# Attention by spectra: context relative to its last row, float32r pair spectra of the two halves, a new order on TensorE

## The chip, the cores and the metric

One core of a Trainium2 chip. A core has five instruction streams: TensorE (PE: matrix products; its weight loads are PEld), VectorE (DVE), ScalarE (ACT), GpSimd (POOL) and SyncE (SP), which here only issues transfers. The metric is device time in microseconds; runs of the same program agree within about 0.05% here. Products land in PSUM, eight banks of 128 x 512 fp32.

## The reference

Inputs: x and a context, both (8, 512, 2048), a 2048 x 2048 weight with bias, and low-rank adapters.

1. q = layernorm(x). In 8 heads of 256 positions each, for every column: corr = ifft(fft(q) * conj(fft(ctx))).real along the positions, its 12 largest lags, a softmax of them, and out[pos] = sum over lags of weight * ctx[min(lag + pos, last)]. The first line of the result is x + out.
2. y = x + layernorm(x) @ W + bias + adapters, in a second stage.

The clipped index min(lag + pos, last) makes positions beyond the end read the last row of the context again. The kernel computes the sum over lags as a second correlation, over a sequence of twice the length: the context, and behind it its last row repeated.

```
w, idx = top_k(corr, topk); w = softmax(w)
for i in range(topk):
    g = minimum(idx[..., i] + pos, L - 1)
    out = out + w[..., i] * take_along_axis(v, g, axis=2)
```

## The kernel before

After a short first stage come the attention stage (some 1,750 us) and the feed-forward stage (some 1,560 us).

**Attention stage.** The work is 32 groups, four to a batch, of 512 positions x 512 columns. All transforms are products with tables: a sequence is folded (sum and difference of its halves) and each fold multiplied with a cosine and a sine table. Four kinds of spectra result, ER, EI, OR and OI (even and odd frequencies, real and imaginary), one PSUM bank each. For one group:
- `fold_v`, `fold_z` (L493 to 509, GpSimd): the folds of the context, and of its second half with the last row (`vrow`, loaded 128 times over).
- `v_spectrum`, `z_spectrum` (L756, L774, TensorE): 8 fp32 products of 512 columns each, through `forward` (L742); v goes to banks 0 to 3, z to 4 to 7. `store_spectrum` (L627, ScalarE) keeps them in `spe` and `spo`.
- `normalise`, `fold_q`, `high_of_q`, `rest_of_q`: q is normalised, folded and cut into two f16 parts; `q_spectrum` (L765) is 24 f16 products.
- `corr_products_even/odd` (VectorE, q spectra times v spectra), `corr_sums` (GpSimd), `turn_row` (ScalarE, one row's sign), `correlation` (L805, TensorE, 16 fp32 products of 256 columns), `corr_to_sbuf` (ScalarE).
- `top_lags` (L958, VectorE): two sums, maxima and replacements for the largest lags; `exponentials`, `sums_of_top`, `divide_w` on ScalarE between; at the end four `wd` products, the weights by lag.
- `transpose_w` (L783), `transposed_out` and `w_rest` (two f16 parts), `weight_spectra` (L793, 48 f16 products into all eight banks), `out_products` (L925, VectorE, nine products in two halves), `out_sums` (L534, GpSimd), `output` (L818, 16 fp32 products of 512 columns), `add_output` (L989).

Each engine runs a step n, one group's share, in an order written out by hand; nothing plans it, and engines meet only through semaphores. A step handles group n and, ahead of it, parts of groups n+1, n+2 and n+3. TensorE (L830): q of n+1, transposes of n, z of n+1, weight spectra of n, correlation of n+1, v of n+2, output of n. VectorE (L996): `w_rest` n, correlation products n+1, row statistics, [weight rest, half 0], output products n, `top_lags` n+1, `add_output` n, [weight rest, half 1, or the largest weight]. The parts in brackets are the side work of the feed-forward weight: in steps 0 to 15 VectorE finds its largest value (L883), in steps 16 to 31 ("convert") it is turned into two f16 parts. For that ScalarE casts (`weights_high`, L681), VectorE subtracts (`weights_rest`, L874), and SP stores both parts and loads the next half (L449 to 459); there is one buffer `wc`. A GpSimd operation and a VectorE operation that reads two SBUF tiles do not run at the same time in this trace, which the rows of line 876 below show by their lengths.

SP (L435) issues every transfer in one order as well, and a wait in it holds up what is behind it: inputs for n+3, the row for the statistics, in the convert steps the two weight stores and loads, then after `out_add` the store of the group's result, its landing, and the load of the next residual.

**Feed-forward stage.** 32 tiles of 128 rows. Per tile: statistics (VectorE), normalise (ScalarE), transposes, the adapters and 192 f16 products of 512 columns (TensorE), the bias added by GpSimd (`prepare`, L1140), and results added by VectorE.

## Time and profile before

| | |
|---|---|
| median of three runs | 3445.23 us (3444.69 to 3445.47) |
| the profiled execution, its time | 3438.6 us |
| its span, first to last instruction | 3436.8 us |
| mean granted TensorE clock | 0.983 |
| busy TensorE, VectorE, ScalarE, GpSimd | 3280.5, 2006.3, 931.3, 1574.0 us |

Busy times are sums over both stages. TensorE's records overlap, since a product is entered before the one ahead of it has drained, so the distance between two starts is the cost of a product, not the length of its record. An fp32 product has two records. What a change in a stage is worth is read from the stage's own timeline, which is why nearly all the rows below are of single groups.

### The profile page before, as it was taken

What the parts mean: (1) busy time and instruction counts of PE and PEld (TensorE: products, weight loads), DVE (VectorE), ACT (ScalarE), POOL (GpSimd) and SP (SyncE); (2) the same over time, 40 slices, a digit from 0 to 9 for tenths busy, and PEclk for the clock granted to TensorE, in tenths of its full rate; (3) what the DMA queues carried; (4) which work ended last, traced back from release to release, by engine and by line L of the source; (5) the groups of instructions that cost most, each with busy time, mean ns of one, the idle gap of its engine ahead of it and who ended that gap; (6) DMA issues with size and microseconds to landing.
All of it is one profiled execution on the core that took longest, in us unless ns stands there. A gap on an engine that the chain in (4) does not pass through costs nothing. (4 is left out here: it accounts for less than half of the span.)

```text
span 3436.8 us, 38078 instructions
## 1 busy us (share of the span) xinstructions
PE 3280.5 (95%) x14592; PEld 1639.7 (48%) x14592; DVE 2006.3 (58%) x2768; ACT 931.3 (27%) x1559; POOL 1574.0 (46%) x727
## 2 busy tenths in 40 slices
PE   7699999999999999999995999999999999999999
PEld 4354554554544455455542444444444444444444
DVE  4289989999888999998985232232323232232321
ACT  1434444344334444544432110111101110111100
POOL 0587888878868888887862110111001110111000
PEclk9799999999999999999998999999999999999999
DMA  7133243342342334234223611011110111011110
GB/s 310 70 113 132 98 153 110 119 153 100 129 152 108 140 127 177 103 126 147 84 101 124 228 50 59 37 38 59 50 54 29 59 49 59 37 38 59 50 50 25
DMA packets 125328, 335.59 MB, mean 98 GB/s; under 512 B 7648, under 2 KB 24160, under 8 KB 108800
## 3 DMA queue, kind: packets, MB, share of 16 engines
q1 hardware_dynamic: 125184, 333.64, 27.1%
q8 instruction: 94, 1.54, 0.2%
q14 instruction: 50, 0.41, 0.0%
HBM read 245.27 MB, written 88.34 MB: 97 GB/s over the span
## 5 line engine op out<-in xcount | busy, mean ns | idle before, releaser
L1248 PE MATMUL ps<-w_hi,h_hi 128*128 128x512 f16 x2048 | 780.0, 381 | 18.4 <-issue 16.9
L1250 PE MATMUL ps<-w_hi,h_lo 128*128 128x512 f16 x2048 | 779.1, 380 | 0.0
L1249 PE MATMUL ps<-w_lo,h_hi 128*128 128x512 f16 x2048 | 778.9, 380 | 0.0
L1143 POOL TENSOR_TENSOR rp<-ve,half 128x1 f32<-128x1 f32 x32 | 17.6, 549 | 1243.7 <-DVE ve L1301 1243.7
L1355 DVE SCALAR_TENSOR_TENSOR xt<-ps,w_back,xt 128x512 f32<-128x512 f32 x128 | 96.0, 750 | 757.1 <-PE ps L1250 756.1
L826 PE MATMUL ps<-op,it 128*128 128x512 f32 x1024 | 448.1, 596 | 21.0 <-DVE op L956 21.0
L752 PE MATMUL ps<-wt,fp 128*128 128x512 f16 x1536 | 339.1, 381 | 9.9 <-ACT spo L639 6.9
L1248 PEld LDWEIGHTS ps<-w_hi,h_hi 128*128 128x128 f16 x2048 | 200.9, 98 | 258.0 <-issue 27.2
L826 PEld LDWEIGHTS ps<-op,it 128*128 128x128 f32 x1024 | 195.7, 191 | 267.8 <-issue 262.3
L1250 PEld LDWEIGHTS ps<-w_hi,h_lo 128*128 128x128 f16 x2048 | 201.0, 98 | 243.9 <-issue 3.9
L1249 PEld LDWEIGHTS ps<-w_lo,h_hi 128*128 128x128 f16 x2048 | 201.0, 98 | 228.9 <-issue 3.3
L1179 ACT ACTIVATE axT<-ps 128x128 f16<-128x128 f32 x32 | 8.9, 277 | 884.4 <-PE ps L1253 884.4
L752 PEld LDWEIGHTS ps<-wt,fp 128*128 128x128 f16 x1536 | 150.7, 98 | 203.2 <-issue 20.4
L814 PE MATMUL ps<-it,cp 128*128 128x256 f32 x1024 | 232.7, 386 | 9.3 <-DVE vlast L946 5.3
L745 PE MATMUL ps<-cg,ft 128*128 128x512 f32 x512 | 230.2, 592 | 0.0
L814 PEld LDWEIGHTS ps<-it,cp 128*128 128x128 f32 x1024 | 194.3, 192 | 50.8 <-DVE vlast L946 15.8
L541 POOL TENSOR_TENSOR mr<-mr 128x1024 f32<-128x1024 f32 x64 | 151.3, 2364 | 142.1 <-DVE mr L940 142.1
L545 POOL TENSOR_TENSOR op<-mr 128x512 f32<-128x512 f32 x64 | 204.7, 3198 | 0.0
L1147 POOL TENSOR_TENSOR xt<-xt,brow 128x2048 f32<-128x2048 f32 x32 | 144.6, 4520 | 103.0 <-ACT h L1163 84.3
L647 ACT ACTIVATE eo<-ps 128x512 f32<-128x512 f32 x128 | 76.4, 597 | 356.8 <-PE ps L814 356.8
L752 PE MATMUL ps<-qh,fp 128*128 128x512 f16 x512 | 155.7, 386 | 12.5 <-DVE wd L986 8.5
L745 PEld LDWEIGHTS ps<-cg,ft 128*128 128x128 f32 x512 | 97.3, 190 | 122.7 <-issue 122.7
(149 smaller groups left out, 5235.3 us busy)
## 6 DMA issues: line engine op xcount, KB each, us to landing
cg<-ctx SPq DMA_DIRECT2D x32, 1024.0 KB, 7.1
xg<-x SPq DMA_DIRECT2D x32, 1024.0 KB, 9.5
xv<-x SPq DMA_DIRECT2D x32, 1024.0 KB
x_scratch<-xv SPq DMA_DIRECT2D x32, 1024.0 KB, 7.4
xt<-x_scratch SPq DMA_DIRECT2D x32, 1024.0 KB, 5.0
out<-xt SPq DMA_DIRECT2D x32, 1024.0 KB, 4.8
xrow<-x SPq DMA_DIRECT2D x24, 1024.0 KB, 5.8
xrow<-w SPq DMA_DIRECT2D x16, 1024.0 KB, 11.3
```

The source lines that it names most:

```text
L541: nc.gpsimd.tensor_tensor(mr[:, 0:2, :], mr[:, 0:2, :], mr[:, 2:4, :], ALU.add).then_inc(pair_sum, 1)
L545: nc.gpsimd.tensor_tensor(op[:, 0, r, :], mr[:, 0, :], mr[:, 1, :], ALU.add).then_inc(op_sum, 1)
L647: nc.scalar.activation(eo[:, j, :], ps[:, TURN[j], :], ACT.Copy).then_inc(corr_out, 1)
L745: last = nc.tensor.matmul(ps[:, bank, :], ft[:, k, kind, :], src[k], start=(k == 0), stop=(k == 1))
L752: last = nc.tensor.matmul(ps[:, bank, :], fp[:, tab, k, kind, :], pair[val][:, 2 * part + k, :], start=(k == 0 and i == 0), stop=(k == 1 a ...
L814: last = nc.tensor.matmul(ps[:, TURN[j], h * HALF:(h + 1) * HALF], cp[:, s, j * P:(j + 1) * P], it[:, s, :], start=(i == 0), stop=(i == 1))
L826: last = nc.tensor.matmul(ps[:, 4 + t, :], it[:, s, (t % 2) * P:(t % 2 + 1) * P], op[:, t // 2, s, :], start=(s == 0), stop=(s == 3))
L1147: nc.gpsimd.tensor_tensor(xt[:, t % 2, :], xt[:, t % 2, :], brow[:, :], ALU.add).then_inc(bias_ok, 1)
L1248: nc.tensor.matmul(ps[:, c, :], h_hi[:, k, i, :], w_hi[:, i, cols], start=(i == 0), stop=False)
L1249: nc.tensor.matmul(ps[:, c, :], h_hi[:, k, i, :], w_lo[:, i, cols], start=False, stop=False)
L1250: last = nc.tensor.matmul(ps[:, c, :], h_lo[:, k, i, :], w_hi[:, i, cols], start=False, stop=(i == KT - 1))
L1355: nc.vector.scalar_tensor_tensor(out=xt[:, k, cols], in0=ps[:, c, :], scalar=w_back[:, 0:1], in1=xt[:, k, cols], op0=ALU.mult, op1=ALU.add ...
```

## The change

It recasts the context mathematics, changes the number format of its transforms, and reorders all five streams in the attention stage.

- The context is taken relative to its last row (`subtract_row`, GpSimd), so the repeated tail becomes zero and needs no term of its own; the last row itself is added back to x in the feed-forward stage (`prepare`: a GpSimd addition of 128 x 2048 for each tile, and a 1 MB load of the row for each batch, `load_last`). `vlast` and its three small operations and its load go.
- Instead of spectra of the folds v and z there are spectra of the two halves, c of the second and a of the first. Each value and each table entry is held as a float32r part (`uh`, `fth`) and a float32r rest (`cgl`, in the place of `cg`; `ftl`), and `forward_u` makes three float32r products where `forward` made one fp32 product. `mix_v` (VectorE, inside `top_lags`) makes the spectrum of v from the two.
- The folding on GpSimd (four operations) becomes two subtractions and two rests; ScalarE gets the two casts `high_of_u` and loses one `store_spectrum`.
- The PSUM halves: `near(g)` and `far_side(g)` are banks 0 to 3 and 4 to 7, or the reverse in odd groups.
- TensorE's order is now transposes n, q n+1, weight spectra n, correlation n+1, c and a of n+2, output n. GpSimd's, ScalarE's and SP's orders change as the diff shows, `weights_high` of half 0 and the second weight store among them.
- In steps 0 to 15 the largest weight is replaced by a sum of magnitudes on ScalarE.

The core of the diff, in the order SP, GpSimd, ScalarE, TensorE, VectorE, feed-forward, its indentation cut:

```diff
+cg_at = -(-nc.sbuf_base // 32) * 32
 cg = sb("cg", [P, 2, TT, GC], FP32, mid)
+cgl = nc.alloc_sbuf_tensor_at("cgl", [P, 2, TT, GC], F32R, offset=cg_at)
...
+def step(b, g, more, lead, far, last, rows, convert):
     n = GPB * b + g
-    if more:
-        sp.wait_ge(z_spec, 4 * n + 8)
-        load_inputs(sp, *ahead(b, g, 3))
+    if far:
+        load_row(*ahead(b, g, 3))
+        load_query(*ahead(b, g, 3))
     if not convert:
         sp.wait_ge(row_used, n + 1)
         sp.dma_start(xrow[:, :], w_t[n]).then_inc(s_wx, 16)
-        sp.wait_ge(wx_used, n + 1)
-    if rows:
-        if convert:
-            sp.wait_ge(row_used, n + 1)
+    elif rows:
+        sp.wait_ge(row_used, n + 1)
         nb, nt = ahead(b, g, 1)
         sp.dma_start(xrow[:, :], x_g[nb + 2, :, nt, :]).then_inc(s_xrow, 16)
     if convert:
-        for h in range(2):
-            m = piece(b, g, h)
-            sp.wait_ge(wch_ok, m + 1)
-            sp.wait_ge(wcl_ok, m + 1)
-            half_cols = slice(h * (D // 2), (h + 1) * (D // 2))
-            sp.dma_start(w_pair_b[0, b - B // 2, g, :, half_cols], wch[:, :]).then_inc(s_wst, 16)
-            sp.dma_start(w_pair_b[1, b - B // 2, g, :, half_cols], wcl).then_inc(s_wst, 16)
-            if h == 0 or lead:
-                sp.wait_ge(s_wst, 32 * m + 32)
-                load_weights(*((b, g, 1) if h == 0 else (*ahead(b, g, 1), 0)))
-    if more:
-        load_row(*ahead(b, g, 3))
+        store_weights(b, g, 0)
+        sp.wait_ge(s_wst, 32 * piece(b, g, 0) + 32)
+        load_weights(b, g, 1)
+    if not last:
+        load_context(*ahead(b, g, 4))
+    if not convert:
+        sp.wait_ge(wx_used, n + 1)
+        nb, nt = ahead(b, g, 1)
+        sp.dma_start(xrow[:, :], x_g[nb + 2, :, nt, :]).then_inc(s_xrow, 16)
     sp.wait_ge(out_add, 4 * n + 4)
     sp.dma_start(x2_g[b, :, :, g * GC:(g + 1) * GC], xv[:, :, :]).then_inc(s_st, 16)
     if lead:
         sp.wait_ge(s_st, 16 * n + 16)
         load_residual(*ahead(b, g, 1))
+    if convert:
+        store_weights(b, g, 1)
+        if lead:
+            sp.wait_ge(s_wst, 32 * piece(b, g, 1) + 32)
+            load_weights(*ahead(b, g, 1), 0)
...
+def subtract_row(b, g):
+    for h in (1, 0):
+        nc.gpsimd.tensor_tensor(cg[:, k, 2 * h:2 * h + 2, :], cg[:, k, 2 * h:2 * h + 2, :], row, ALU.subtract).then_inc(u_sub, 1)
+def rest_of_u(b, g):
+    m, k = GPB * b + g, g % 2
+    for i, h in enumerate((1, 0)):
+        pool.wait_ge(u_hi, 2 * m + i + 1)
+        nc.gpsimd.tensor_tensor(cgl[:, k, 2 * h:2 * h + 2, :], cg[:, k, 2 * h:2 * h + 2, :], uh[:, 2 * h:2 * h + 2, :],
+                                ALU.subtract).then_inc(u_lo, 1)
...
-def step(b, g, more, lead, rows):
+def step(b, g, more, lead, far, rows):
     if more:
-        fold_v(*ahead(b, g, 2))
+        rest_of_u(*ahead(b, g, 2))
         fold_q(*ahead(b, g, 2))
-        rest_of_q(*ahead(b, g, 2))
     if lead:
         corr_sums(*ahead(b, g, 1))
     out_sums(b, g)
-    if more:
-        fold_z(*ahead(b, g, 2))
     if rows and g == GPB - 1:
         next_rows(b)
-fold_v(0, 0)
+    if more:
+        rest_of_q(*ahead(b, g, 2))
+    if far:
+        subtract_row(*ahead(b, g, 3))
...
+def high_of_u(b, g):
+    m, k = GPB * b + g, g % 2
+    if later(b, g):
+        act.wait_ge(a_spec, 4 * m)
+    for i, h in enumerate((1, 0)):
+        act.wait_ge(u_sub, 2 * m + i + 1)
+        nc.scalar.activation(uh[:, 2 * h:2 * h + 2, :], cg[:, k, 2 * h:2 * h + 2, :], ACT.Copy).then_inc(u_hi, 1)
...
+def sum_of_weights(b, g):
+    n = GPB * b + g
+    act.wait_ge(s_wx, 16 * n + 16)
+    nc.scalar.activation(xrow[:, :], xrow[:, :], ACT.Abs, accum_out=wsum[:, bass.ds(n, 1)]).then_inc(wx_used, 1)
 def step(b, g, more, lead, far, convert):
     n = GPB * b + g
     transposed_out(b, g)
+    if convert:
+        weights_high(b, g, 0)
     if more:
         high_of_q(*ahead(b, g, 2))
     if lead:
-        store_spectrum(*ahead(b, g, 1), 1)
-    if convert:
-        weights_high(b, g, 0)
-    if lead:
         turn_row(*ahead(b, g, 1))
         corr_to_sbuf(*ahead(b, g, 1))
+    if more:
+        store_c(*ahead(b, g, 2), True)
     if convert:
         weights_high(b, g, 1)
-    if more:
-        act.wait_ge(oprod, 9 * n + 9)
-        store_spectrum(*ahead(b, g, 2), 0)
+    else:
+        sum_of_weights(b, g)
+    if far:
+        normalise(*ahead(b, g, 3))
     if lead:
-        exponentials(*ahead(b, g, 1))
+        exponentials(*ahead(b, g, 1), more)
         sums_of_top(*ahead(b, g, 1))
         divide_w(*ahead(b, g, 1))
     if far:
-        normalise(*ahead(b, g, 3))
+        high_of_u(*ahead(b, g, 3))
...
+def forward_u(bank, kind, k, part):
+    for r in range(2):
+        row = 2 * part + r
+        for i, (tab, val) in enumerate(((fth, uh[:, row, :]), (ftl, uh[:, row, :]), (fth, cgl[:, k, row, :]))):
+            last = nc.tensor.matmul(ps[:, bank, :], tab[:, r, kind, :], val, start=(r == 0 and i == 0), stop=(r == 1 and i == 2))
...
+def a_spectrum(b, g):
+    m, k = GPB * b + g, g % 2
+    pe.wait_ge(u_lo, 2 * m + 2)
+    if later(b, g) and later(b, g - 1):
+        pe.wait_ge(oprod, 8 * m - 8)
+    elif later(b, g):
+        pe.wait_ge(cprod, 4)
+    for i in range(4):
+        forward_u(far_side(g) + i, i, k, 0).then_inc(a_spec, 1)
...
 def q_spectrum(b, g):
     m, k = GPB * b + g, g % 2
     pe.wait_ge(q_lo, 2 * m + 2)
-    pe.wait_ge(v_out, 4 * m + 4)
+    if not (later(b, g) and later(b, g - 1)):
+        pe.wait_ge(c_out, 4 * m + 4)
     for i in range(4):
-        if later(b, g):
-            pe.wait_ge(w_ready, 4 * m - 3 + i)
-        forward_pair(i, i, (qh, ql[k]), i // 2).then_inc(q_spec, 1)
...
 def weight_spectra(b, g, lead):
     n = GPB * b + g
+    pe.wait_ge(wt_lo, 4 * n + 4)
+    for i in range(4):
+        forward_pair(near(g) + i, (ER, EI)[i % 2], (wt[:, 0], wt[:, 1]), i // 2).then_inc(w_spec, 1)
     if lead:
         pe.wait_ge(cprod, 4 * n + 8)
-    pe.wait_ge(wt_lo, 4 * n + 4)
     for i in range(4):
-        forward_pair(i, (ER, EI)[i % 2], (wt[:, 0], wt[:, 1]), i // 2).then_inc(w_spec, 1)
-    if lead:
-        pe.wait_ge(z_out, 4 * n + 8)
-    for i in range(4):
-        forward_pair(4 + i, (OR, OI)[i % 2], (wt[:, 0], wt[:, 1]), i // 2).then_inc(w_spec, 1)
+        forward_pair(far_side(g) + i, (OR, OI)[i % 2], (wt[:, 0], wt[:, 1]), i // 2).then_inc(w_spec, 1)
 def correlation(b, g):
     m = GPB * b + g
     pe.wait_ge(cp_turn, m + 1)
+    if later(b, g):
+        pe.wait_ge(oprod, 8 * m - 4)
+    else:
+        pe.wait_ge(v_add, 4)
...
+def output(b, g, more, lead):
+    pe.wait_ge(hi_sum, 2 * n + 2)
+    if lead and not more:
+        pe.wait_ge(corr_out, 4 * n + 8)
+        if more:
+            pe.wait_ge(c_out, 4 * n + 8 + (1, 3, 4, 4)[TURN[t]])
+        pe.wait_ge(op_sum, 6 * n + (4 if t > 1 else 6))
...
 def step(b, g, more, lead):
+    transpose_w(b, g)
     if lead:
         q_spectrum(*ahead(b, g, 1))
-    transpose_w(b, g)
-    if lead:
-        z_spectrum(*ahead(b, g, 1))
     weight_spectra(b, g, lead)
     if lead:
         correlation(*ahead(b, g, 1))
     if more:
-        v_spectrum(*ahead(b, g, 2))
-    output(b, g)
+        c_spectrum(*ahead(b, g, 2))
+        a_spectrum(*ahead(b, g, 2))
+    output(b, g, more, lead)
...
+def mix_v(b, g):
+    m, k, bank = GPB * b + g, g % 2, far_side(g)
+    dve.wait_ge(c_out, 4 * m + 4)
+    dve.wait_ge(a_spec, 4 * m + 4)
+    nc.vector.tensor_tensor(spe[:, k, 0, 0::2, :], ps[:, bank + ER, :].unsqueeze(1).broadcast_to([P, 2, GC]),
+                            spe[:, k, 1, 0::2, :], ALU.add).then_inc(v_add, 1)
+    nc.vector.scalar_tensor_tensor(out=spe[:, k, 0, 1, :], in0=ps[:, bank + EI, :], scalar=nyq[:, 0:1],
+                                   in1=spe[:, k, 1, 1, :], op0=ALU.mult, op1=ALU.add).then_inc(v_add, 1)
+    nc.vector.tensor_tensor(spo[:, k, 0, :, :], ps[:, bank + OR:bank + OI + 1, :], spo[:, k, 1, :, :],
+                            ALU.subtract).then_inc(v_add, 1)
+    dve.wait_ge(v_add, 4 * m + 1)
+    nc.vector.tensor_tensor(spe[0:1, k, 0, 2, :], ps[0:1, bank + EI, :], spe[0:1, k, 1, 2, :], ALU.add).then_inc(v_add, 1)
...
+    if nxt:
+        mix_v(*nxt)
...
-def step(b, g, lead, rows, convert):
+def step(b, g, more, lead, rows, convert):
     w_rest(b, g)
     if lead:
-        corr_products_even(*ahead(b, g, 1))
-        corr_products_odd(*ahead(b, g, 1))
+        corr_products(*ahead(b, g, 1))
     if rows:
         row_statistics(b, g)
     if convert:
         weights_rest(b, g, 0)
     out_products(b, g, lead)
     if lead:
-        top_lags(*ahead(b, g, 1))
+        top_lags(*ahead(b, g, 1), ahead(b, g, 2) if more else None)
     add_output(b, g)
     if convert:
         weights_rest(b, g, 1)
-    else:
-        largest_weight(b, g)
...
+def load_last(b):
+    sp.dma_start(vl[:, :], ctx[b, L - 1, :].partition_broadcast(P)).then_inc(s_vl, 16)
...
+        if t == TT - 2 and not (isinstance(b, int) and b == B - 1):
+            sp.wait_ge(vl_ok, TT * b + TT)
+            load_last(b + 1)
...
 def prepare(b, t):
-    n = TT * b + t
+    n, k = TT * b + t, t % 2
+    pool.wait_ge(s_xt[k], 16 * (2 * b + t // 2 + 1))
+    pool.wait_ge(s_vl, 16 * b + 16)
+    nc.gpsimd.tensor_tensor(xt[:, k, :], xt[:, k, :], vl[:, :], ALU.add).then_inc(vl_ok, 1)
     pool.wait_ge(ve_ok, n + 1)
```

## Rows read from the trace of the kernel before

**Rows 1.** The page: busy us, share of the span and instructions of each engine.
```profile
PE 3280.5 (95%) x14592; PEld 1639.7 (48%) x14592; DVE 2006.3 (58%) x2768; ACT 931.3 (27%) x1559; POOL 1574.0 (46%) x727
```

**Rows 2.** Timeline, TensorE, one group of the first half: start, length, what, idle before.
```profile
692.87 1.91 PE L790 MATMUL ps<-ident,wd 128*128 128x128 f32 x16
695.10 3.67 PE L745 MATMUL ps<-zs,ft 128*128 128x512 f32 x8 [0.32 <-DVE wt L922]
...
702.04 10.52 PE L752 MATMUL ps<-wt,fp 128*128 128x512 f16 x48
712.55 7.17 PE L814 MATMUL ps<-it,cp 128*128 128x256 f32 x32
719.56 3.60 PE L745 MATMUL ps<-va,ft 128*128 128x512 f32 x8
...
726.43 13.90 PE L826 MATMUL ps<-op,it 128*128 128x512 f32 x32
740.25 0.59 PE L752 MATMUL ps<-qh,fp 128*128 128x512 f16 x2
...
745.43 1.91 PE L790 MATMUL ps<-ident,wd 128*128 128x128 f32 x16
```

**Rows 3.** Timeline, TensorE, one group of the second half, transposes to transposes.
```profile
1290.16 1.91 PE L790 MATMUL ps<-ident,wd 128*128 128x128 f32 x16
...
1343.27 1.91 PE L790 MATMUL ps<-ident,wd 128*128 128x128 f32 x16
```

**Rows 4.** Timeline, VectorE, a group of each half.
```profile
696.66 1.22 DVE L865 TENSOR_TENSOR mr<-ps,spe 128x1024 f32<-128x1024 f32 x1
...
707.42 2.29 DVE L940 TENSOR_TENSOR mr<-ps,spe 128x2048 f32<-128x2048 f32 x1 [3.47 <-PE ps L752]
...
711.83 0.67 DVE L946 SCALAR_TENSOR_TENSOR vlast<-ps,vlast 1x512 f32<-1x512 f32 x1
...
713.56 1.20 DVE L951 TENSOR_TENSOR mhi<-ps,spe 128x1024 f32<-128x1024 f32 x1
715.81 2.29 DVE L940 TENSOR_TENSOR mr<-ps,spo 128x2048 f32<-128x2048 f32 x1 [1.06 <-POOL op L545]
...
741.87 2.48 DVE L993 SCALAR_TENSOR_TENSOR xv<-ps,xv 128x512 f32<-128x512 f32 x4
...
1302.18 2.83 DVE L876 SCALAR_TENSOR_TENSOR wc<-wc,w_scale,wch 128x1024 f16<-128x1024 f32 x1 [0.38 <-ACT wch L686]
...
1342.10 1.28 DVE L876 SCALAR_TENSOR_TENSOR wc<-wc,w_scale,wch 128x1024 f16<-128x1024 f32 x1
```

**Rows 5.** Timeline, GpSimd: the two correlation sums of a group.
```profile
701.42 2.36 POOL L531 TENSOR_TENSOR cp<-mr 128x1024 f32<-128x1024 f32 x1 [0.47 <-DVE mi L872]
703.73 2.35 POOL L532 TENSOR_TENSOR cp<-mi 128x1024 f32<-128x1024 f32 x1
```

**Rows 6.** Timeline of the first correlation, and stretches behind it; granted clock third from the end.
```profile
135.59 8.86 PE L814 MATMUL ps<-it,cp 128*128 128x256 f32 x32 [3.51 <-ACT cp L625]
...
135.60:137.60 2.00, 2.00 (x6) 1.68 (x7) 0.00 (x0) 0.00 (x0) 2.00 (x2) 0.67 1.04 398
137.60:140.00 2.40, 2.40 (x8) 1.91 (x7) 0.00 (x0) 0.60 (x1) 2.40 (x2) 0.56 0.70 259
```

**Rows 7.** SP: a weight store and the next load; landing times of lines 463 and 433.
```profile
1343.45 0.32 SPq L455 DMA_DIRECT2D w_pair_scratch<-wch  x1
...
1346.15 0.33 SPq L433 DMA_DIRECT2D wc<-w  x1
...
DMA to landing us min/median/max: 4.6/7.4/9.8
...
DMA to landing us min/median/max: 3.1/3.6/5.8
```

**Rows 8.** Timeline, ScalarE: the weight cast.
```profile
1301.01 1.14 ACT L686 ACTIVATE wch<-wc,w_scale 128x1024 f16<-128x1024 f32 x1
```

**Rows 9.** Timeline, GpSimd, feed-forward stage: the bias addition.
```profile
2540.58 4.51 POOL L1147 TENSOR_TENSOR xt<-xt,brow 128x2048 f32<-128x2048 f32 x1 [2.73 <-ACT h L1163]
```

More of the change, by code:

```diff
@@ L25 @@
 FP16 = mybir.dt.float16
+F32R = mybir.dt.float32r
 U32 = mybir.dt.uint32
@@ L418, in build, with near, far_side @@
             wcl_ok = sem("wcl_ok", st)
+            def near(g):
+                return 4 * (g % 2)
+            def far_side(g):
+                return 4 - 4 * (g % 2)
             with nc.Block() as block:
@@ L666, in divide_w @@
                     def divide_w(b, g):
-                        m = GPB * b + g
+                        m, bank = GPB * b + g, near(g)
                         act.wait_ge(rz_ok, m + 1)
@@ L720, in _ @@
                     corr_to_sbuf(0, 0)
-                    store_spectrum(0, 1, 0)
-                    exponentials(0, 0)
+                    store_c(0, 1, False)
+                    normalise(0, 2)
+                    exponentials(0, 0, True)
                     sums_of_top(0, 0)
                     divide_w(0, 0)
-                    normalise(0, 2)
+                    high_of_u(0, 2)
                     for g in range(GPB):
@@ L741, in _ @@
                 def _(pe):
-                    def forward(bank, kind, src):
-                        for k in range(2):
-                            last = nc.tensor.matmul(ps[:, bank, :], ft[:, k, kind, :], src[k], start=(k == 0), stop=(k == 1))
+                    def forward_u(bank, kind, k, part):
[3 more added lines that the diff above has]
+                                last = nc.tensor.matmul(ps[:, bank, :], tab[:, r, kind, :], val, start=(r == 0 and i == 0), stop=(r == 1 and i == 2))
                         return last
```

276 lines of the change are left out of this document (138 added, 138 removed).

## The prediction

> **What bounds the kernel now.** I read the page first: TensorE is busy 95% of the span and VectorE 58% [rows 1]. Those shares mix two stages, so the timeline of one group of the attention stage comes next, engine by engine. On TensorE the reader is to see no hole: transposes start at 692.87 and again at 745.43, a period of 52.56 us, and inside it only 0.32 us of waiting [rows 2]. The pieces are q 5.18 (745.43 - 740.25), transposes 1.91, z 6.94, weight spectra 10.51, correlation 7.01, v 6.87, output 13.82. In the half that also converts weights the period is 53.11 [rows 3]. So the attention stage is TensorE-bound by a hair: VectorE is nearly full too, and its chain hides by about a microsecond. The feed-forward stage is TensorE alone.
>
> **What the change takes from TensorE.** z and v are 16 fp32 products of 512 columns: 13.81 us, 0.86 each, four passes of 0.216. A 512-column f16 product takes 0.216 too: 48 of them are the 10.51 of the weight spectra [rows 2]. New are 48 float32r products (24 for c, 24 for a). No row shows float32r. Lower bound: the f16 rate, 10.4 us a group, 3.4 saved. Upper bound: the fp32 rate, 41 us, 28 lost. I take the lower: it is a third of the rows' own decomposition, three single products in place of four passes, and the fp32 transposes, one pass each, need 1.91/16 = 0.12 us with their 128 weight rows, so a 4-byte weight load fits behind a 0.216 us product [rows 2]. The Trainium skill ("FP8 and Floating Point Precision", "TensorE Precision Notes") says that true FP32 takes four passes and that reduced-precision FP32 is 4-byte data truncated on reading; by it one pass each is right, and no run here shows it yet.
>
> So TensorE's own work becomes 1.91 + 5.18 + 10.4 + 7.01 + 10.4 + 13.82 = 48.7 us a group.
>
> **What the new order does.** Take S as the start of the transposes. Transposes end at 1.9, q at 7.1, weight spectra at 17.45. Before, z stood between, and q a whole output earlier, so q's products were out of VectorE's way. Now:
> - q's last bank is ready at 7.1; the last two of the four correlation products (1.13 each, [rows 4]) end at 9.6.
> - GpSimd's two correlation sums start 0.1 later, 2.32 each [rows 5]: 14.4. Row statistics on VectorE (2.75) hide there.
> - The first four output products reuse mr and mi and wait for these sums: 14.4 + 6.7 = 21.1. The 6.7 is from 707.42 to the end of the row of 713.56, less the 0.6 of vlast, which goes [rows 4].
> - The correlation now waits for all four, because it goes into the banks they read. It starts at 21.2, not 17.45: TensorE waits 3.75 us. Before it needed only the first three for its first two banks, which ended near the end of the weight spectra.
> - From there 7.0 + 10.4 + 13.8 = 31.2: the next transposes at 52.4.
>
> VectorE's chain ends beside it. The second-half products start 8.4 after the first ones (GpSimd's sums between, 707.42 to 715.81): 22.8. From there to the last wd the old trace takes 26.06 (715.81 to 741.87); less 0.6 for the removed row sum, plus mix_v. mix_v is two PSUM-and-SBUF operations of 1024 elements and two of 512 or fewer: 2 x 1.13 + 2 x 0.6 = 3.5 by the products' rows [rows 4]; its bounds are 2.3 and 5. Sum 51.7, 0.7 short of the 52.4. Were that cover gone, each microsecond more on VectorE is one more in the period. The moved largest-weight reduction (2.28 on VectorE to ScalarE) lies off both chains. GpSimd's own count is unchanged (four folds become two subtractions and two rests), about 44 of 52 us. So of the 3.9 us taken from TensorE nearly all comes back as the wait: first half 52.4 against 52.56.
>
> **The clock.** After a wait of 3.51 us the old correlation took 8.86 us instead of 7.17, with the granted clock at 0.67 and 0.56 in the next 4.4 us, so at the lower level (1.2 GHz) for most of it [rows 6]. A wait of 3.75 may bring that in each group or only in some: 0 to 1.7 us, I take 0.7 in the first half (period 53.1 to 53.2). In the second the wait is double, and I take the full price. The Trainium skill ("TensorE: Matmul & The Clock Gate", "HAM oscillation") has the throttle return at waits between bursts, each time round the loop. The trace agrees with its 1.7 us. By the rule all first-half groups pay, period 54.1, which would be 14 us more in the sum; without it 11 less.
>
> **The second half: the weight conversion.** Two orders change together. ScalarE casts weight half 0 right behind the transposed copies, ahead of high_of_q and turn_row; before it stood behind them. And SP sends weight half 1 of the group before only after the output store has landed and the residual load is issued; before it sent it first, and the next load went out 2.7 us after [rows 7]. Now, from S:
> - add_output ends at 1.8; its store lands after 4.6 to 9.8 us, median 7.4 [rows 7]. I take 4.7, as the transfers that ran beside it are no longer there: 6.6.
> - Residual load issued, then the two stores of weight half 1, 7.1 to 7.9, behind its megabyte. Alone they take 2.7 with issue; with that megabyte, at 2 to 7, I take 4.5: 12.1.
> - Load of the next half, 3.1 to 5.8, median 3.6, taken as 3.4 [rows 7]: 15.5. ScalarE cast 1.05 [rows 8]: 16.6. VectorE's rest, 1.2 when free (1.28 at 1342.10; 2.83 at 1302.18, when a GpSimd sum was in its way [rows 4]): 17.9.
> - Output products only then: 24.6. Correlation at 24.7, a wait of 7.25. Plus 31.2: 55.9.
> - With the low clock the correlation ends 1.7 later; VectorE has then finished its output additions 0.9 earlier against S, and the store chain gives that back: 56.7.
> Bounds of this period: 54.1, if weights come in time and only the rest (waiting 2 us behind the correlation sums, then 1.2) stands in front of the products; 61.7, with the store at 7.2, the weight stores at 7 and the clock.
>
> What queues behind the late cast: on ScalarE high_of_q (GpSimd's rest_of_q wants it only after its output sums, covered) and turn_row, without which the correlation can't start. turn_row would then be done at 16.6 + 2.0 + 0.6 = 19.2, ahead of the products' 24.6, so VectorE's side decides. Behind the late store on SP stand the loads of the row and of x for three groups on; they go out at 12.4 to 13.3 and are wanted at about 39, when ScalarE normalises ahead of the exponentials. In the first half SP's moved wait for the sum of magnitudes holds back only the row for the next statistics, wanted some 20 us later, and the context load, wanted a group later. These moves I put at nothing; were the x load later than 39, normalise would push the exponentials, and with them the 0.7 us of VectorE's cover.
>
> **Ends.** Start: the first c spectrum waits for GpSimd operations in a new order, three folds of 2.35 more than the first v (7 us) [rows 5]; later steps give some back and mix_v of group 1 adds 3.5: +7, between +4 and +9. Feed-forward: each tile gets a GpSimd addition of 128x2048, 4.51 us by the bias addition [rows 9], between the landing and the statistics. It stands bare in the first tile (+5); afterwards the tile ahead covers it, with the new row load beside the tile's own once a batch and the adapter loads once a batch; in those two tiles of four I expect up to a microsecond to show (an estimate; no row has such a tile), +5, between 0 and the addition's full 4.5 in one tile of each but the first few batches, 16. The removed last-row load and vlast operations were hidden.
>
> **Sum.** 16 periods of the first half x (+0.7) = +11; 14 of the second x (56.7 - 53.1 = 3.6) = +50; start +7; feed-forward +10. Together +78 on the profiled execution's 3438.6 us (span 3436.8): 3517. The median of the runs is 6.6 above that execution, so 3523.
>
> **Rivals.**
> 1. Faster: the correlation doesn't wait. If its release comes 3.75 us sooner than I lay it out (products or sums that overlap more than their rows say, a weight load that is never late), TensorE's 48.7 decides: -3.8 x 16, -4.4 x 14, less the +17 of the ends: -106, 3340. It decides from a release before 17.45. For it: TensorE had no hole before. Against: every step of the chain is a semaphore wait and its row hardly varies. Chance 0.11.
> 2. float32r costs two passes: 0.43 each, +10.4 a group on the path behind the correlation. 30 periods give +310, with the rest of my sum +365 or so: 3800 (at four passes 4430). For it: no row. Against: the argument by passes. Chance 0.12.
> 3. The weight load is in time. Second half at 54.1, clock mostly up: +14, first half -3 to +11, ends +10: 3470. For it: the stores and loads are short when alone. Against: three landings now stand in series before a ScalarE queue. Chance 0.11, part of it within 0.2% of now.
> 4. My forecast, 0.66. Its own range is 3485 to 3600.
>
> Low end: second half 54.1, first 52.4, ends at their lower bounds: +17, 3462. High end: 61.7 in the second half (+120), 54.1 in the first (+25), ends +25: +170, 3620. Rivals 1 and 2 stay outside. About 0.2% (7 us) is what a measurement of this kernel tells from no change. Faster 0.11 (rival 1), same 0.06 (the low part of 3), slower 0.83.
>
> **What would show it.** c and a: 24 products each in 5.2 us. In each group a hole in front of the correlation, 3.8 us in the first half, released by VectorE's mhi product, and about 7 in the second, where ScalarE's weight cast waits for the weights' DMA and turn_row stands behind it. A granted clock under 1 in the first microseconds of the correlation. No hole before the transposes over 0.5 us. I am wrong if the holes are absent, if they stand before the transposes (VectorE's chain then bounds), or if float32r rows are longer than f16's.

## The result, and the profile after

The changed kernel takes 3628.62 us (median of four runs, 3625.42 to 3633.91) against 3444.96 us for the kernel before beside it: a ratio of 1.0538, 95% interval 1.052 to 1.0557, so 5.4% slower. The profiled execution took 3626.31 us, its span is 3624.5 us. The forecast was 3523 us with a range of 3462 to 3620: the sign is right, and the size is 106 us short. Executions of one kernel differ by more than the 0.05% that I gave for the kernel before: by 0.23% here, and by 0.46% (3441.44 to 3457.16 us) for the kernel before beside the first experiments. All times are medians of four executions (seven for the kernel before beside the experiments); one execution of e6 took 19,035 us, for which the record shows no cause, and without it e6's median would be 3706.89 in place of 3708.33.

The mean granted clock fell from 0.983 to 0.951. The page's busy times, and its group for the correlation (busy us, mean ns of one, idle time before and what ended it):

```profile
PE 3245.0 (90%) x15104; PEld 1780.6 (49%) x15104; DVE 2123.8 (59%) x2817; ACT 928.1 (26%) x1528; POOL 1679.4 (46%) x759
...
L871 PE MATMUL ps<-it,cp 128*128 128x256 f32 x1024 | 295.4, 459 | 216.2 <-DVE mhi L1014 207.7
```

Against [rows 1], TensorE is busy 36 us less and the span is 188 us longer. TensorE now waits 216 us ahead of the correlation, nearly all for `mhi`, VectorE's fourth output product.

TensorE's timeline over one group of the first half, from transposes to transposes, answers to [rows 2]:

```profile
677.51 1.97 PE L847 MATMUL ps<-ident,wd 128*128 128x128 f32 x16 [1.61 <-DVE wd L1050]
...
684.49 10.52 PE L810 MATMUL ps<-wt,fp 128*128 128x512 f16 x48
698.79 8.86 PE L871 MATMUL ps<-it,cp 128*128 128x256 f32 x32 [3.77 <-DVE mhi L1014]
707.30 0.58 PE L803 MATMUL ps<-uh,fth 128*128 128x512 f32 x1
...
733.63 0.55 PE L847 MATMUL ps<-ident,wd 128*128 128x128 f32 x3 [1.32 <-DVE wd L1050]
```

Stretches of the correlation (granted clock third from the end of a row; the later two have 1.00) answer to [rows 6]:

```profile
698.80:701.20 2.40, 2.40 (x9) 2.05 (x10) 0.85 (x1) 0.00 (x0) 2.40 (x3) 0.79 0.00 0
701.20:703.60 2.40, 2.40 (x8) 1.84 (x7) 2.40 (x2) 0.60 (x1) 2.40 (x3) 0.50 0.00 0
```

The period is 56.12 us, where it was 52.56. There are two holes, and the second, ahead of the transposes, was not forecast: it says that VectorE's chain ends last, which is one of the signs by which the prediction said that it would be wrong. The same group on VectorE, from the upper output products to `wd`:

```profile
700.35 2.29 DVE L1007 TENSOR_TENSOR mr<-ps,spo 128x2048 f32<-128x2048 f32 x1 [1.62 <-POOL op L578]
...
707.02 2.09 DVE L1016 TENSOR_TENSOR op<-mhr 128x512 f32<-128x512 f32 x1
709.03 1.78 DVE L1018 TENSOR_TENSOR op<-mhi 128x512 f32<-128x512 f32 x1
710.73 2.31 DVE L1025 TENSOR_TENSOR cr<-eo 128x1024 f32<-128x1024 f32 x1
712.97 3.17 DVE L1026 TENSOR_TENSOR cr<-eo 128x1024 f32<-128x1024 f32 x1
...
731.09 2.48 DVE L1050 SCALAR_TENSOR_TENSOR wd<-eo,ps 128x512 f32<-128x512 f32 x4 [0.80 <-ACT ps L717]
```

Four sums take 9.15 us (707.02 to 716.14). In the kernel before there were five, the addition of the context's last row first, and they took 5.6 us:

```profile
722.48 2.08 DVE L952 TENSOR_TENSOR op<-op,vlast 1x512 f32<-1x512 f32 x1
724.49 0.67 DVE L954 TENSOR_TENSOR op<-mhr 128x512 f32<-128x512 f32 x1
725.09 0.67 DVE L956 TENSOR_TENSOR op<-mhi 128x512 f32<-128x512 f32 x1
725.69 1.21 DVE L963 TENSOR_TENSOR cr<-eo 128x1024 f32<-128x1024 f32 x1
726.83 1.21 DVE L964 TENSOR_TENSOR cr<-eo 128x1024 f32<-128x1024 f32 x1
...
723.96 5.20 POOL L545 TENSOR_TENSOR op<-mr 128x512 f32<-128x512 f32 x1
```

GpSimd's record of 5.20 us is an operation that takes 1.27 when nothing is in its way: it was held up while VectorE ran four sums. In the changed kernel each operation of GpSimd gets in between two sums, as its records in that stretch show:

```profile
706.18 2.38 POOL L576 TENSOR_TENSOR mi<-mi 128x1024 f32<-128x1024 f32 x1
708.51 1.75 POOL L578 TENSOR_TENSOR op<-mr 128x512 f32<-128x512 f32 x1
...
711.92 3.14 POOL L557 TENSOR_TENSOR xg<-qa,qh 128x1024 f16<-128x1024 f32 x1
```

These sums read two operands from SBUF, and so do GpSimd's. That such a pair keeps each other waiting is a rule of the Trainium skill ("SBUF — State Buffer", "Who interferes with whom"): an operation of VectorE with two SBUF inputs contends with a GpSimd operation that reads SBUF. The trace agrees. The same section says that issue order, and not the shape of an operation, decides who blocks; who is next when both stand in line it doesn't say, and there e3 and e6 below, which put operations of different shape in the same place, differ.

The second half, one group of the weight conversion, TensorE, then ScalarE and SyncE (answering to [rows 3, 7, 8]):

```profile
1381.87 1.97 PE L847 MATMUL ps<-ident,wd 128*128 128x128 f32 x16 [0.49 <-DVE wd L1050]
...
1408.30 9.76 PE L871 MATMUL ps<-it,cp 128*128 128x256 f32 x32 [8.91 <-DVE mhi L1014]
...
1443.12 1.09 PE L847 MATMUL ps<-ident,wd 128*128 128x128 f32 x8 [0.42 <-DVE wd L1050]
...
1399.11 1.15 ACT L732 ACTIVATE wch<-wc,w_scale 128x1024 f16<-128x1024 f32 x1 [14.25 <-DMA wc<-w]
...
1384.24 0.40 SPq L491 DMA_DIRECT2D x_scratch<-xv  x1
1388.43 0.37 SPq L455 DMA_DIRECT2D xv<-x  x1
1388.90 0.45 SPq L465 DMA_DIRECT2D w_pair_scratch<-wch  x1
...
1395.79 0.33 SPq L458 DMA_DIRECT2D wc<-w  x1
```

Period 61.25 us (59.8 to 63.6 in steps 17 to 29), hole 8.91 us. SyncE's chain is the one forecast: output store, residual load, weight stores, the next load, and ScalarE waits for it.

The difference of the two spans, 187.7 us, by the starts of the transposes:

| stretch | before | after | more |
|---|---|---|---|
| up to the first transposes | 166.8 | 171.8 | +5.0 |
| steps 0 to 15 | 841.2 | 898.5 | +57.3 |
| step 16 | 70.7 | 65.8 | -5.0 |
| steps 17 to 29 | 690.4 | 800.2 | +109.8 |
| step 30 | 50.0 | 56.4 | +6.4 |
| from the last transposes on | 1617.7 | 1631.9 | +14.1 |

### The profile page after: what moved, and what is told of

Read it like the earlier page. It is cut to its first block and busy times, and to the rows that moved or that the text cites. A ratio compares the mean times of both kernels' runs of the same rounds, so it can differ in the third digit from the quotient of the medians.

```text
span 3624.5 us, 39388 instructions
## 1 busy us (share of the span) xinstructions
PE 3245.0 (90%) x15104; PEld 1780.6 (49%) x15104; DVE 2123.8 (59%) x2817; ACT 928.1 (26%) x1528; POOL 1679.4 (46%) x759
## 5 line engine op out<-in xcount | busy, mean ns | idle before, releaser
L1218 POOL TENSOR_TENSOR xt<-xt,vl 128x2048 f32<-128x2048 f32 x32 | 144.2, 4505 | 1015.9 <-DMA xt<-x_scratch 746.7
L871 PE MATMUL ps<-it,cp 128*128 128x256 f32 x1024 | 295.4, 459 | 216.2 <-DVE mhi L1014 207.7
L871 PEld LDWEIGHTS ps<-it,cp 128*128 128x128 f32 x1024 | 238.8, 237 | 275.8 <-DVE mhi L1014 175.7
L541 POOL TENSOR_TENSOR cgl<-cg,uh 128x1024 fp32r<-128x1024 f32 x64 | 162.8, 2567 | 328.8 <-ACT uh L662 321.4
L803 PE MATMUL ps<-uh,fth 128*128 128x512 f32 x512 | 206.6, 404 | 28.7 <-POOL cgl L541 28.7
L1373 DVE BATCH_NORM_STATS2 bn<-xt 128x6 f32<-128x512 f32 x128 | 79.1, 681 | 231.2 <-POOL xt L1218 231.2
L803 PE MATMUL ps<-cgl,fth 128*128 128x512 f32 x512 | 200.6, 392 | 0.0
L803 PE MATMUL ps<-uh,ftl 128*128 128x512 f32 x512 | 200.3, 391 | 0.0
```

Of the source, the lines that this page charges most:

```text
L541: nc.gpsimd.tensor_tensor(cgl[:, k, 2 * h:2 * h + 2, :], cg[:, k, 2 * h:2 * h + 2, :], uh[:, 2 * h:2 * h + 2, :], ALU.subtract).then_inc(u ...
L803: last = nc.tensor.matmul(ps[:, bank, :], tab[:, r, kind, :], val, start=(r == 0 and i == 0), stop=(r == 1 and i == 2))
L871: last = nc.tensor.matmul(ps[:, far_side(g) + j, h * HALF:(h + 1) * HALF], cp[:, s, j * P:(j + 1) * P], it[:, s, :], start=(i == 0), stop= ...
L1218: nc.gpsimd.tensor_tensor(xt[:, k, :], xt[:, k, :], vl[:, :], ALU.add).then_inc(vl_ok, 1)
```

## The experiments

Twelve kernels in three sets. In each set the kernel before was measured beside them, with a median between 3443.96 and 3445.47 us.

| run | edit | us | ratio to before, 95% |
|---|---|---|---|
| e1 | changed + weight stores early on SyncE | 3575.15 | 1.0341 to 1.0403 |
| e2 | changed + correlation split | 3658.68 | 1.0581 to 1.0647 |
| e3 | changed + addition of a zero row | 3583.05 | 1.0362 to 1.0422 |
| e4 | before, row addition left out | 3603.51 | 1.0413 to 1.0474 |
| e5 | e1 + e3 | 3525.06 | 1.0215 to 1.0249 |
| e6 | changed + an operation on 128 partitions there | 3708.33 | 1.0737 to 1.078 |
| e7 | e5 + VectorE's waits cut | 3428.79 | 0.9936 to 0.9969 |
| e8 | e7 + e2 | 3385.53 | 0.9811 to 0.9844 |
| e9 | before + the same two waits cut | 3425.72 | 0.992 to 0.9965 |
| e10 | e8 without the zero row | 3542.37 | 1.026 to 1.031 |
| e11 | changed + the zero row behind two sums | 3604.04 | 1.043 to 1.0478 |
| e12 | as e6 on 64 partitions | 3602.03 | 1.0432 to 1.048 |

**e1, SyncE's order.**

```diff
                         if not last:
                             load_context(*ahead(b, g, 4))
+                        if convert:
+                            store_weights(b, g, 1)
+                            if lead:
+                                sp.wait_ge(s_wst, 32 * piece(b, g, 1) + 32)
+                                load_weights(*ahead(b, g, 1), 0)
...
                             load_residual(*ahead(b, g, 1))
-                        if convert:
...
```

> SyncE sends the stores of weight half 1 and the next load of half 0 ahead of the output wait and the x2 store again, as the kernel before did; all else is the changed kernel. Theory (the second half's extra comes from the order of SyncE's issues): the cast on ScalarE has its weights some 5 us earlier, the 8.7 to 11.2 us hole ahead of the correlation shrinks to the 3.8 us of the first half or a little more, and the second-half period goes from 61.6 to 56 to 58 us; over 13 to 14 groups that is 50 to 75 us, so 3555 to 3580 us. Rival (the cast ahead of the row that is turned is the trouble, wherever the load is issued, or VectorE's uncut chain and its port set the period): the period stays above 60 us and the time above 3610 us.

Measured: 53 us less than the changed kernel, with 58.0 us a group in the second half (1365.35 to 1423.35). The cast comes 10.5 us behind the start of the transposes instead of 17.2, and the hole is 5.65 us. The theory holds, and the first half stays at 56.1. What is left over the first half's 3.77 is VectorE's weight rest of half 0, now next in line, at 3.31 us where it took 1.28 at 1400.29 in the changed kernel:

```profile
1378.49 3.31 DVE L948 SCALAR_TENSOR_TENSOR wc<-wc,w_scale,wch 128x1024 f16<-128x1024 f32 x1
```

**e2, the correlation split.** The correlation begins in the two banks that are free after two of VectorE's four products; the copies of its banks, and the waits for them, follow in the same order.

```diff
-                            pe.wait_ge(oprod, 8 * m - 4)
...
+                                pe.wait_ge(oprod, 8 * m - (6 if j < 2 else 4))
...
-  last = nc.tensor.matmul(ps[:, far_side(g) + j, h * HALF:(h + 1) * HALF], ...
+  last = nc.tensor.matmul(ps[:, far_side(g) + TURN[j], h * HALF:(h + 1) * HALF], ...
```

> The correlation writes its banks in the order 2, 3, 0, 1 of its half again and waits for two, then four of the first output products, as before the change; the context spectra wait for the copies of the bank they write. Theory A (VectorE's chain bounds the first half at 56.1 us): the 3.77 us hole ahead of the correlation goes or falls to under 0.5 us, but as much comes back ahead of the transposes (now 1.3 to 1.6 us, then 5 to 7), and the first-half period stays within 0.5 us of 56.1; time within 15 us of 3628. Theory B (TensorE's hole and the lower clock behind it bound it): the period falls by 3 us or more in the 16 first-half groups, 3575 us or less. In the second half both leave the hole, since the cast holds the row that the correlation reads.

Measured: 30 us slower than the changed kernel, which neither theory had; theory A had it within 15. In the first half the hole ahead of the correlation shrank to 1.5 us and the correlation took 7.17 us, its length at full clock, but the hole ahead of the transposes grew to 5.38:

```profile
577.72 3.68 PE L847 MATMUL ps<-ident,wd 128*128 128x128 f32 x16 [5.38 <-DVE wd L1050]
...
598.66 7.17 PE L871 MATMUL ps<-it,cp 128*128 128x256 f32 x32 [1.51 <-DVE mi L1010]
```

So VectorE's chain bounds (theory A), and with a price: the transposes now run at the lower clock (3.68 us for 1.97), and VectorE waits for them, whereas the correlation, at 8.86 us or at 7.17, was not what it waited for. A stretch from 577.70 to 581.20 had a granted clock of 0.50, the lower of the two levels (1.2 GHz). The first-half periods went to between 56.0 and 59.0 us.

**e3 and e4, the row addition.** It goes back into the changed kernel with a row of zeros, and comes out of the kernel before.

```diff
+  nc.vector.tensor_tensor(op[0:1, 1, ER, :], op[0:1, 1, ER, :], zrow[:, :], ALU.add).then_inc(hi_sum, 1)
   dve.wait_ge(oprod, 8 * n + 7)
```

> An addition of a row of zeros on one partition stands ahead of VectorE's two upper-half sums, where the kernel before had its own row addition; nothing else differs from the changed kernel. Theory A (the short operation is what lets VectorE keep the port, so that its sums run one behind the other and GpSimd waits): the four sums take 4 to 6 us instead of 9.1, VectorE's chain gets 3 us shorter, and the first-half period falls from 56.1 to between 54 and 55, where TensorE's own chain with its hole takes over: 15 to 40 us over the kernel, 3585 to 3612 us. Theory B (who gets the port follows from when the sums and GpSimd's operations meet): VectorE and GpSimd still alternate, each sum takes 1.8 to 3.2 us, and the added 0.7 to 2 us make the period up to 1 us longer: 3628 to 3650 us.

> The kernel before, with its addition of the context's last row to one output spectrum left out (that part of the result is missing); VectorE goes from the last product straight to the upper-half sums. Theory A (the short operation held the port for VectorE): the sums and the additions behind them now alternate with GpSimd and take 8 to 9 us in place of 5.6, as in the changed kernel; VectorE had some 3.5 us to spare ahead of the transposes, so that the period moves by 0 to 1 us: 3440 to 3460 us. Theory B: the sums still run one behind the other at 0.67 us and 1.21 us while GpSimd's operation is held for 3 to 5 us, and the time stays within 5 us of 3441.

Measured: an operation more made the changed kernel 46 us faster, and one less made the kernel before 158 us slower. VectorE in e3:

```profile
751.79 2.09 DVE L1016 TENSOR_TENSOR op<-op,zrow 1x512 f32<-1x512 f32 x1
753.81 0.67 DVE L1018 TENSOR_TENSOR op<-mhr 128x512 f32<-128x512 f32 x1
...
756.15 1.21 DVE L1028 TENSOR_TENSOR cr<-eo 128x1024 f32<-128x1024 f32 x1
```

and in e4, with TensorE behind it; the first line is from another group:

```profile
544.41 13.73 DVE L953 TENSOR_TENSOR op<-mhr 128x512 f32<-128x512 f32 x1
...
725.11 2.08 DVE L953 TENSOR_TENSOR op<-mhr 128x512 f32<-128x512 f32 x1
...
731.00 3.36 DVE L963 TENSOR_TENSOR cr<-eo 128x1024 f32<-128x1024 f32 x1
...
746.58 0.59 PE L752 MATMUL ps<-qh,fp 128*128 128x512 f16 x2 [3.60 <-DVE wd L985]
```

On the cause theory A is right both ways. In e3, at 3583 us 2 us below its range, the period is 54.57 us, no hole is left ahead of the transposes, and TensorE's own chain with its hole of 3.77 bounds. In e4 I had the size wrong (at most 3460 us against 3603.51): I gave VectorE 3.5 us to spare ahead of the transposes, but the q spectrum stands there and waits for `wd`. The sums took 9.25 us for 5.55. The 3.7 us came out as a hole of 3.60, and q behind it ran 1.7 us longer: 57.9 us in place of 52.56. Neither theory had what happened in two groups of e4: VectorE's first sum took 13.73 us (the line of 544.41) while GpSimd, after the operation that it had under way, ran six more one behind the other at their usual lengths (545.89 to 557.59), and then VectorE's other three ran at 0.68, 1.21 and 1.21 us. The periods there are 65.0 and 65.4 us. So GpSimd can keep the turn too, and taking turns one by one is not the only order that two-input sums without the short operation meet.

**e5, both together.**

> The changed kernel with SyncE's weight stores ahead of the output wait (as in e1_store_order) and the addition of a row of zeros ahead of VectorE's upper-half sums (as in e3_row_add). Theory (two separate costs, one of SyncE's order, one of the port): in the first half the period is that of e3, 54.6 us, in the second half the 58.0 us of e1 less the 3.2 to 3.6 us by which the sums get shorter, 54.5 to 55; with 3575 us for e1 that is 3490 to 3515 us. Rival (the gains overlap, since TensorE's hole ahead of the correlation remains in both): the second-half period stays above 56.5 us and the time above 3535 us.

Measured: 50 us less than e1, where e3 gave 46, so the two gains add up and the rival falls, but 10 us above my range: the second-half periods are 55.2 to 57.3, since the hole of 4.6 to 5.6 us ahead of the correlation and its 8.6 to 10.2 us remain. No hole stands ahead of the transposes.

**e6, e11 and e12, what the short operation does.** e6 puts `tensor_tensor(x, x, x, max)` on 128 partitions where e3 has its row, e12 the same on 64; e11 puts the row of zeros between the second and the third sum.

> The changed kernel with one operation ahead of VectorE's upper-half sums, in the place of e3's row of zeros, but on all 128 partitions (each element the maximum of itself and itself, in place). Theory A (it is the operation on a single partition that lets VectorE keep the port): VectorE and GpSimd alternate as in the changed kernel, with one more sum to wait for, 1.7 to 2.3 us more in a chain that bounds: period 57.5 to 58.5 us in the first half, 3670 to 3710 us. Theory B (any operation issued there without a wait of its own does it): the sums behind it run at 0.67 and 1.21 us, and the time is that of e3, 3575 to 3595 us.

> The changed kernel with the addition of the row of zeros between VectorE's two upper-half sums and the two additions of the correlation, in place of ahead of all four. Theory (VectorE keeps the port from the short operation on): the two sums ahead of it still alternate with GpSimd (2.1 and 1.8 us), the short one waits for one more operation, and the two behind it take 1.21 us each; the chain is 1 to 1.5 us shorter than in the changed kernel, where TensorE's chain allows 1.5: 3590 to 3610 us. Rival (only an operation at the head, or the number of them, matters): the two behind it take 2.3 and 3.2 us, and the time is 3640 us or more.

> As e6_row_wide, on the first 64 partitions in place of all 128. If VectorE keeps the port only behind an operation on one or few partitions, this run is as e6 (3690 to 3720 us, the sums 1.8 to 3.2 us each); if any operation on fewer than 128 partitions does it, it is as e3 (3575 to 3595 us, the sums 0.67 us).

Measured, VectorE in e6, e11 and e12:

```profile
795.26 2.07 DVE L1015 TENSOR_TENSOR op<-op 128x512 f32<-128x512 f32 x1
797.26 1.78 DVE L1017 TENSOR_TENSOR op<-mhr 128x512 f32<-128x512 f32 x1
...
803.76 3.17 DVE L1027 TENSOR_TENSOR cr<-eo 128x1024 f32<-128x1024 f32 x1
```

```profile
649.04 1.77 DVE L1020 TENSOR_TENSOR op<-op,zrow 1x512 f32<-1x512 f32 x1
650.74 1.21 DVE L1027 TENSOR_TENSOR cr<-eo 128x1024 f32<-128x1024 f32 x1
```

```profile
643.86 2.07 DVE L1015 TENSOR_TENSOR op<-op 64x512 f32<-64x512 f32 x1
645.85 1.78 DVE L1017 TENSOR_TENSOR op<-mhr 128x512 f32<-128x512 f32 x1
647.56 1.78 DVE L1019 TENSOR_TENSOR op<-mhi 128x512 f32<-128x512 f32 x1
649.26 1.21 DVE L1026 TENSOR_TENSOR cr<-eo 128x1024 f32<-128x1024 f32 x1
```

The times are 3708, 3604 and 3602 us: e6 and e11 lie in the ranges of the theories (e6 with first-half periods up to 60.4 us, above the 58.5 forecast), and e12 between its two answers.

An operation on all partitions does nothing but wait in turn (e6): the two sums behind it take 1.78 us each in every group, and the two additions 3.17 us in 24 of 31 groups and 1.21 in the other seven; in six of these GpSimd has the two small operations for the statistics in its order there. One on a single partition waits at most once, for the operation that GpSimd has under way, and VectorE's operations right behind it run through (e3, e5, e8, e9, e11 and the kernel before, in all 31 groups of each). They do so only while VectorE doesn't pause. In three groups of e7, which has the row of zeros too, VectorE waited some 0.15 to 1.3 us for ScalarE ahead of the additions, and from there on the turns came back:

```profile
562.98 0.67 DVE L1026 TENSOR_TENSOR op<-mhi 128x512 f32<-128x512 f32 x1
563.75 2.15 DVE L1033 TENSOR_TENSOR cr<-eo 128x1024 f32<-128x1024 f32 x1
565.82 3.42 DVE L1034 TENSOR_TENSOR cr<-eo 128x1024 f32<-128x1024 f32 x1
```

64 partitions give something between: two sums still take turns, two run through, and GpSimd is held for 4.88 us. That fits neither of my answers. e3 and e6 also differ in more than the partitions (an addition of another tile against a maximum of one operand with itself); only e6 and e12 change the partitions alone. So "a single partition" is what was seen, not the rule behind it; the rule stays open.

**e7, e8 and e10, VectorE's chain cut.** The edits of e7 beside those of e5 (the first weight rest also moves behind the first four products, and each upper product waits only for the sum that frees its own buffer):

```diff
-                                dve.wait_ge(cp_sum, 2 * n + (4 if lead else 2))
+                                dve.wait_ge(cp_sum, 2 * n + (3 if lead else 2))
...
-                            pool.wait_ge(oprod, 8 * n + 4 * h + 2)
-                            nc.gpsimd.tensor_tensor(mi[:, 0:2, :], ...
                             pool.wait_ge(pair_sum, 4 * n + 2 * h + 1)
                             nc.gpsimd.tensor_tensor(op[:, 0, r, :], ...
+                            pool.wait_ge(oprod, 8 * n + 4 * h + 2)
+                            nc.gpsimd.tensor_tensor(mi[:, 0:2, :], ...
```

> As e5_order_and_row, and VectorE's chain is cut where the changed kernel lets it wait for GpSimd: the first output product waits for the first of the two correlation sums alone (it reuses only that buffer), GpSimd adds and stores each real part before the imaginary pair, so that the upper product's first buffer is free 1.6 us earlier, and the first weight rest comes behind the first four output products. Theory (VectorE's chain and the hole behind it are the bound): 2.2 and 1.6 us less on VectorE, and the fourth product ends 2.2 us earlier, so that TensorE's hole ahead of the correlation shrinks from 3.77 to 1.5 us; period 50.5 to 52.4 us in the first half, 51.5 to 54 in the second: 3400 to 3460 us, beside or below the kernel before. Rival (GpSimd's own order or the load of the port takes it back): period above 53.5 us, above 3475 us.

> As e7_chain, with the correlation split as in e2_corr_split. Theory: with VectorE's chain cut, the rest of TensorE's hole (1.5 us) and the lower clock behind it are now what bounds, so that here the split helps by 0.5 to 2 us per group: 3370 to 3440 us and 15 to 60 us less than e7. Rival (the hole only moves ahead of the transposes, as it did in e2): within 10 us of e7 or slower.

> As e8_chain_split, without the addition of a row of zeros ahead of VectorE's upper-half sums. Theory (the port's price is paid wherever VectorE's chain bounds): the four sums take 8 to 9.5 us again, the first-half period goes from 48.8 (TensorE's own work) to 51 to 52.5, the second-half one from 51.5 to 54.5 to 55.5; 3455 to 3490 us. Rival (with VectorE's chain cut by 4 us, the sums meet other operations of GpSimd and no longer alternate, or have room): 3380 to 3410 us.

Measured: in the first half e7 has 50.8 us in its plain groups, with a hole of 1.66 and a correlation of 7.17, and 52.8 to 55.6 in those where it is 3.64 to 3.73; its second half has 50.8 to 51.6 in most groups and 57.7 to 58.2 in two. e8 has 48.8 in the first half, and 50.5 in those. Its plain group is TensorE without a hole, at a granted clock of 1.00:

```profile
666.05 1.91 PE L848 MATMUL ps<-ident,wd 128*128 128x128 f32 x16
...
683.34 7.07 PE L872 MATMUL ps<-it,cp 128*128 128x256 f32 x32
...
701.15 13.90 PE L886 MATMUL ps<-op,it 128*128 128x512 f32 x32
714.88 1.36 PE L848 MATMUL ps<-ident,wd 128*128 128x128 f32 x11
```

The cuts of VectorE's chain gave 96 us (e5 to e7), and the split that cost 30 us in e2 gives 43 more here, because TensorE's hole now bounds. e8 is 1.7% faster than the kernel before. Its second half has 51.2 to 51.8 us in most groups and 55.7 in two, with VectorE's chain at the end (holes of about 1.9 ahead of the transposes). e10 is 157 us slower than e8, where I gave 70 to 105: the sums took 8.2 us against 4.3 (578.88 to 587.04, and 546.02 to 550.37 in e8), and the hole came ahead of the transposes, 3.2 to 3.6 us in the first half and up to 6.5 in the second, with slow transposes behind it in many groups of the first half and in all of the second (3.68 us, as in e2): 52.3 to 56.0 us in the first half, 58 in the second.

**e9, the same cuts before the change.**

> The kernel before, with the two edits of VectorE's chain that e7_chain had and that exist in it too: the first output product waits for the first correlation sum alone, and GpSimd adds and stores each real part ahead of the imaginary pair. Theory (the kernel before is bound by TensorE, busy 52.24 of a group's 52.56 us at full clock, so VectorE's chain has little to give there): period 52.2 to 52.6 us in both halves and 3425 to 3450 us. Rival (VectorE's chain bounds before as well): 1 us less per group, 3415 us or less.

Measured: 52.48 us in both halves, 3425.72 us, at the low end of the range. The first half moved by 0.1 us (TensorE bounds); the second lost its 0.6 us a group, and step 16 went from 70.7 to 65.2 us. The rival falls. So of the 59 us by which e8 lies below the kernel before, 18 are to be had without the change, by cuts that fit the kernel before as well; what the change gives with all the cuts is the 40 us from 3425.72 to 3385.53.

## Why the prediction was right or wrong

**Right.** The removed passes: 48 float32r products take 11.1 us and not the 41 of the fp32 rate, so one pass each (rival 2 falls); the price was 0.23 us each and not 0.216, +0.7 a group (their rows are 0.39 to 0.40 us long and the f16 ones 0.38, so that sign of being wrong showed, by little). The hole ahead of the correlation in the first half: forecast 3.75, measured 3.77, released by `mhi`. The start of the upper products: forecast 22.8 us behind the transposes, measured 22.84. `mix_v`: 3.5 us, measured 3.5. The chain behind the cast: output store issued and landed at 6.6 us (6.6), cast and rest in series, period well above the first half's. Start: +7 forecast, +5.0 measured, within its bounds.

**The step that failed: VectorE's chain "less 0.6 for the removed row sum".** I took the operation for its own 0.6 us. What it did was let the four sums behind it run through while GpSimd waited. All five took 5.6 us before; the four alone take 9.15, so the term was +3.6 and not -0.6, as e3 and e4 show from both sides. In the first half VectorE's chain therefore ends at 56.0 and not at 51.7, behind TensorE's, where the prediction had it hidden with 0.7 us to spare. Of the 109 us by which the spans' difference of 187.7 exceeds the +78 forecast, 46 lie in steps 0 to 15, 66 in steps 17 to 30 and 4 behind them; the start and step 16 take 7 back. Putting the operation back gives 46 us (e3), and 50 from e1 to e5; the 53 us that e1 gives back are the price of SyncE's order, for which, with the clock, the forecast had 50.

**Terms mis-sized.** The clock: I took 0.7 of 1.7 us in the first half; every group paid the whole or more (correlation 8.6 to 10.1 us for 7.17, granted clock 0.79 and 0.50 in the first 4.8 us of the one shown). In the changed kernel VectorE's later end hides this. The rule of the Trainium skill that the prediction named ("TensorE: Matmul & The Clock Gate", "HAM oscillation"), with all first-half groups paying, was the better guide. The traces agree: in e3, where VectorE doesn't decide, the period is 54.57, and 52.4 + 1.7 + 0.7 for float32r is 54.8. The weight stores: 6.4 us behind the residual's megabyte (1389.39 to 1395.79), not 4.5; cast at 17.2, not 15.5. With VectorE's sums at the end of the group the period is 61.25 in place of 56.7. The feed-forward: I had +5 at its entry and +5 later. The tiles cost 1.6 us in all: from the first tile's adapter transpose to the last's are 1492.7 us, before 1491.1. The entry cost 5.9 (the transposes' wait 25.02 against 19.13); up to the first tile's adapter transpose 1.3 of it came back. The last group of the attention stage, whose output starts 38.5 us behind the transposes where it was 30.6, cost 7.9: its cast starts 17.3 us behind the transposes, where it was 9.8.

**Rival 1** (no wait, TensorE's 48.7) was false for this kernel, and right on what lies below: e8 runs at 48.83 in its plain groups of the first half.

**Two sums of the prediction** don't come out of their own terms: rival 2 gives 3833 us and not 3800 (+310 and the +78 of the rest), and the high end gives 3615 and not 3620. Neither changes what is said here.

## What to carry to other kernels

Before an operation is taken out of a chain, look at what it keeps away from what stands behind it: read the other engine's records beside it, and one that takes 5.2 us where its kind takes 1.27 is being held up by something. A long hole on TensorE costs twice, as idle time and as a lower clock behind it, and where it stands decides whether the second price is felt: ahead of the transposes it slowed the very chain that was late, ahead of the correlation it did not. With two chains of nearly one length, cutting the one that doesn't end last gives nothing or harms (e2, 30 us slower); once the other had been cut (e7, 96 us faster than e5), the same cut gave 43 us (e8).

## What the runs showed of the hardware

- Who is next when a two-input VectorE operation and a GpSimd operation both wait for SBUF depends on the operation ahead. Behind one on a single partition VectorE's next four operations ran at 0.67, 0.67, 1.21 and 1.21 us, with a GpSimd operation of 1.27 us held for up to 5.25 (e5). They ran through in every group of the kernel before, e3, e5, e8 and e9, and in 28 of 31 groups of e7; in the other three VectorE paused in between. Behind one on 128 partitions the four took 1.78, 1.77, 3.17 and 3.17 in 24 of 31 groups (e6). Without such an operation GpSimd kept the turn through six further operations in two groups of e4, and VectorE waited 13.73 us.
- A float32r product of 512 columns took 0.227 to 0.231 us (48 in 11.11), the f16 one 0.216, the fp32 one 0.86 (before and after).
- Over all fourteen traces, 240 of 243 correlations behind a hole of 3.6 us or more took 8.6 to 10.2 us (the granted clock was 0.79 and then 0.50 in the changed kernel's first 4.8 us); the other three, behind 3.64, 3.73 and 3.77 us, took 7.1 to 7.2. Of 53 behind holes of 1.3 to 3.3 us, 49 took 7.1 to 7.2; the other four, behind 2.27, 2.32, 2.71 and 3.29 us (e7, e8), took 8.6 to 8.9.
